# A sandwich of attention and mixture of experts on one core: three program blocks become one, six padding writes move behind the steering table, and two buffers change address

## The reference, cut to what matters

```python
# layer 1: row sums of exp(q k^T) under a causal mask, then a small MLP
o = exp_qk.sum(axis=-1)                  # one number for each token
o = relu(o @ fc1_w.T + fc1_b) @ fc2_w.T + fc2_b
# layer 2: 8 experts, each token goes to its best 2
logits = flat @ gate_w + gate_b
topv, topi = lax.top_k(logits, 2)
h = gelu(flat @ W1e + b1e); out = h @ W2e + b2e     # 256 -> 1024 -> 256
final += out * routing_weight
```

## Time and profile before

| | |
|---|---|
| time, median of 3 runs | 705.41 us (705.11 to 705.66) |
| the profiled execution: its own time, and its span | 705.67 us, 703.9 us |
| busy: PE, DVE, ACT, POOL | 563.0 (80%), 484.4 (69%), 298.3 (42%), 182.5 (26%) us |
| last input to stage 2's first matmul: last write of `steer` to first W1 matmul | 210.18 to 229.87 us |
| tiles in stage 2 | 36 |
| DMA over the whole span | 66.79 MB, 95 GB/s |

### The profile page before, as it was taken

One profiled execution on the slowest core, in us unless ns is written; L12 is line 12 of the kernel. 1 busy time (PEld: TensorE's weight loads), 2 busy tenths in 40 slices (PEclk: granted clock), 3 DMA queues, 4 the chain that ended last, 5 costly groups with the idle time before them and its releaser, 6 DMA issues. The chain is left out here.

```text
span 703.9 us, 14366 instructions
## 1 busy us (share of the span) xinstructions
PE 563.0 (80%) x4174; PEld 508.2 (72%) x4175; DVE 484.4 (69%) x1571; ACT 298.3 (42%) x673; POOL 182.5 (26%) x153
## 2 busy tenths in 40 slices
PE   2768788684230899999999999999999999999700
PEld 1536373542110899999999999999899999999600
DVE  4988888686450676976666666669766666796547
ACT  3564657564210546533333333358242424653250
POOL 2000170624424231223232323232231313131300
PEclk9958879797565899999999999999999999999955
DMA  9970020211125535632232223246432323433286
GB/s 289 310 269 0 13 102 8 83 38 53 68 70 151 188 46 152 166 44 51 39 51 39 51 39 52 38 115 163 95 45 45 45 45 45 149 55 49 46 274 211
DMA packets 52876, 66.79 MB, mean 95 GB/s; under 512 B 4870, under 2 KB 47340, under 8 KB 52716
## 3 DMA queue, kind: packets, MB, share of 16 engines
q1 hardware_dynamic: 37740, 46.81, 20.9%
q0 software_dynamic: 14016, 18.56, 15.6%
q10 hardware_dynamic: 1088, 1.07, 0.5%
HBM read 38.26 MB, written 28.74 MB: 95 GB/s over the span
## 5 line engine op out<-in xcount | busy, mean ns | idle before, releaser
L1073 ACT ACTIVATE h<-pL,b_now 128x256 f32<-128x256 f32 x288 | 121.0, 471 | 244.7 <-PE pL L1139 243.8
L1052 POOL DMA_INDIRECT sum_y<-y,dest x72 | 115.5, 1605 | 319.7 <-DVE y L1204 308.7
L1139 PE MATMUL pL<-xeT_hi,w_lo 128*128 128x256 f32 x576 | 163.5, 284 | 6.0 <-issue 3.7
L1151 PE MATMUL pY<-w_hi,h_lo 128*128 128x256 f32 x576 | 164.2, 285 | 0.9 <-DVE h_lo L1177 0.7
L1139 PE MATMUL pL<-xeT_hi,w_hi 128*128 128x256 f32 x576 | 162.5, 282 | 0.0
L1139 PE MATMUL pL<-xeT_lo,w_hi 128*128 128x256 f32 x576 | 162.4, 282 | 0.0
L1151 PE MATMUL pY<-w_hi,h_hi 128*128 128x256 f32 x576 | 161.1, 280 | 0.0
L1151 PE MATMUL pY<-w_lo,h_hi 128*128 128x256 f32 x576 | 160.8, 279 | 0.0
L1139 PEld LDWEIGHTS pL<-xeT_hi,w_lo 128*128 128x128 f32 x576 | 109.3, 190 | 7.9 <-issue 4.6
L1151 PEld LDWEIGHTS pY<-w_hi,h_lo 128*128 128x128 f32 x576 | 108.5, 188 | 1.3 <-DVE h_lo L1177 1.3
L1139 PEld LDWEIGHTS pL<-xeT_hi,w_hi 128*128 128x128 f32 x576 | 109.3, 190 | 0.0
(11 more groups left out here) (185 smaller groups left out, 699.1 us busy)
## 6 DMA issues: line engine op xcount, KB each, us to landing
w_stage<-w SPq DMA_DIRECT2D x16, 1024.0 KB, 7.9
xt<-sorted_x SPq DMA_DIRECT2D x38, 260.0 KB, 2.7
sum_y<-fill SPq DMA_DIRECT2D x1, 4352.0 KB, 24.7
w_stage<-sum_y SPq DMA_DIRECT2D x8, 512.0 KB, 5.2
out<-z SPq DMA_DIRECT2D x8, 512.0 KB, 3.0
x_all<-x SPq DMA_DIRECT2D x3, 1024.0 KB, 8.7
sum_y<-y,dest POOLq DMA_INDIRECT x72, 3.8
sorted_x<-fill ACTq DMA_DIRECT2D x4, 260.0 KB, 5.6
```

The source lines that it names most:

```text
L1052: pool.indirect_dma_start(out=sum_y, out_offset=bass.IndirectOffsetOnAxis(ap=dest[:, i:i + 1], axis=0), in_=y[:, i, :], in_offset=None, co ...
L1073: a = act.activation(h[:, c, :], pL[:, bk, i * TM:(i + 1) * TM], ACT.Gelu, bias=b1_now[par][:, c:c + 1])
L1139: mm = pe.matmul(pL[:, bk, i * TM:(i + 1) * TM], w[:, 0, col], x[:, k, :], start=(k == 0 and w is lo), stop=(k == KC - 1 and x is xeT_lo))
L1151: mm = pe.matmul(pY[:, i, 0:D], s[:, c, rows], w[:, 1, c * D:(c + 1) * D], start=(c == 0 and s is h_lo), stop=(c == FC - 1 and w is lo))
```

## The change: what it does

1. One block around all three stages. The DRAINs, gathers and releases at L336 and L999 are gone. In their place each engine waits for what it needs: PE, ACT, DVE, SP and POOL for `steer_ready` = 2 (the table's counts, L808, now increment it too), DVE also for `b2_in`, POOL for `sums_cleared`.
2. SP fills the ends of experts 0 and 1 on `ends_ready`; ACT fills those of experts 2 to 7, after `steer_ready` = 2. Nobody waits for them at once; a late tile's load waits for all 8, beside `rows_sent`.
3. A filler's 256 rows are spread so that each partition writes two neighbouring rows (`(p a)` for `(a p)`), and the ids in `fill` follow.
4. POOL sends all 16 indirect DMAs of the last batch in a row.
5. `fill` and `fwarm` live for the whole program (they were buffers of one stage); `fwarm` grows from 1 to 24 numbers for each partition. `h` is put behind `h_hi` and `h_lo`. By the addresses of the built programs, every large buffer of stages 2 and 3 keeps its address modulo 64 bytes: `w_hi1`, `w_lo1`, `xeT_hi`, `xeT_lo`, `h`, `h_hi`, `h_lo` and `z0` to `z7` were at 0 and are at 0, and the outer `w_stage`, `w_hi0`, `w_lo0`, `xt` stay at 32. In stage 1, `xn`, `xT_hi`, `xT_lo`, `qk`, `rope_a`, `rope_b`, `qkr` and `probs` go from 32 to 0, and `hid`, `hidT`, `x3T`, `logitsT` and most of the routing's small tiles from 0 to 32.

The diff, without the change of indentation and cut to its core:

```diff
+        fill = sb("fill", [P, TM // P, XW], F32)
+        fwarm = sb("fwarm", [P, 24], F32)
...
+        block = ctx.enter_context(nc.Block())
...
-            with nc.Block() as block:
-                def fill_ends(eng, experts, filled):
+            def fill_ends(eng, experts):
                     eng.wait_ge(ends_ready, 1)
                     for e in experts:
                         end = eng.value_load(steer[0:1, C_END + e:C_END + e + 1], ...)
-                        eng.dma_start(sorted_x[bass.ds(end, TM), :].rearrange("(a p) c -> p a c", p=P),
-                                      fill[:]).then_inc(filled, 16)
-                    eng.wait_ge(filled, 16 * len(experts))
+                    eng.dma_start(sorted_x[bass.ds(end, TM), :].rearrange("(p a) c -> p a c", p=P),
+                                  fill[:]).then_inc(ends_filled, 16)
...
-                    fill_ends(sp, range(0, NE, 2), ends_filled)
-                    sp.wait_ge(sums_cleared, 16)
-                    sp.wait_ge(b2_in, 16)
+                sp.sem_inc(ends_filled, ONE)
+                fill_ends(sp, range(SP_ENDS))                      # SP_ENDS = 2
...
-                    send_rows(pool, range(SENT_FIRST))
+                send_rows(pool, range(2 * TB))
...
-                    fill_ends(act, range(1, NE, 2), odd_ends_filled)
+                act.wait_ge(steer_ready, 2)
+                fill_ends(act, range(SP_ENDS, NE))
...
                     def load_tile(sp, word):
                         hold(sp, rows_sent, (word & 1) * BATCH_SENT + (B - 1) * BATCH_SENT, passed)
+                    hold(sp, ends_filled, (word & 1) * END_SENT + ONE, passed)    # END_SENT = NE * 16
...
-                    both = sp.value_load(steer[0:1, C_TILES + NE - 1:C_TILES + NE], ...)
+                sp.wait_ge(steer_ready, 2)
                     load_tile(sp, tile_word(sp, 0))
                     sp.wait_ge(tile_turned, 1)
                     sp.wait_ge(tag_saved, 1)
                     load_tile(sp, tile_word(sp, 1))
+                both = sp.value_load(steer[0:1, C_TILES + NE - 1:C_TILES + NE], ...)
...
-                    send_rows(pool, range(SENT_FIRST, 2 * TB))
+                pool.wait_ge(steer_ready, 2)
+                pool.wait_ge(sums_cleared, 16)
```

More of the change, by code:

```diff
@@ L54 @@
 BATCH_SENT = 2 * TB * 16
-SENT_FIRST = TB
+SP_ENDS = 2
+END_SENT = NE * 16
 RSQRT_LINKS = 10
@@ L931, in build @@
             xeT_lo = se("xeT_lo", [P, KC, TM], F32R)
-            h = se("h", [P, FC, TM], F32)
             h_hi = se("h_hi", [P, FC, TM], F32R)
             h_lo = se("h_lo", [P, FC, TM], F32R)
+            h = se("h", [P, FC, TM], F32)
             tag = se("tag", [P, TM // P, 4], F32)
@@ new lines, in _, with tile, first @@
+            @block.gpsimd
+            def _(pool):
+                pool.sem_inc(y_left, ONE)
+                pool.wait_ge(steer_ready, 2)
+                pool.wait_ge(sums_cleared, 16)
+                def tile(e, par, g):
+                    for i in range(TM // P):
+                        hold(pool, y_ready, 2 * g + i + 1, passed)
+                        pool.indirect_dma_start(
+                            out=sum_y, out_offset=bass.IndirectOffsetOnAxis(ap=dest[:, i:i + 1], axis=0),
+                            in_=y[:, i, :], in_offset=None,
+                            compute_op=ALU.add).then_inc(y_sent, 16)
+                    hold(pool, y_sent, (g + 1) * 32, y_left)
+                def first(e, pair, par, g):
+                    tile(e, par, g)
+                over_tiles(pool, None, first, None, tile)
@@ new lines, in tile @@
+                            for k in range(KC):
+                                col = slice(k * F + c * P, k * F + (c + 1) * P)
+                                for w, x in ((lo, xeT_hi), (hi, xeT_hi), (hi, xeT_lo)):
+                                    mm = pe.matmul(pL[:, bk, i * TM:(i + 1) * TM], w[:, 0, col], x[:, k, :],
+                                                   start=(k == 0 and w is lo), stop=(k == KC - 1 and x is xeT_lo))
+                        mm.then_inc(l1_done, 1)
+                    turn(g + 1)
```

1466 lines of the change are left out of this document (722 added, 744 removed).

## The result

The changed kernel took **700.72 us** (median of 6 runs, 698.63 to 702.19), the kernel before 705.26 (6 runs, 703.76 to 707.39): a ratio of 0.994, 95% interval 0.9925 to 0.9956. It is faster, but by 4.5 us and not by 8.9. The profiled execution took 700.91 us, with a span of 699.1 after 703.9.

The account below looks back on a forecast made before the run. POOL's drain was taken to hold up stage 2's start. 7.56 us at the hand-over and 1.34 at stage 2's end make 8.9, so 705.41 becomes 696.5 us; own range 695.0 to 697.8, 8-in-10 range 694.3 to 699.5.

Parts of the forecast that it names:

- What bounds the kernel: Between stages 1 and 2 all engines wait for POOL's drain, which ends at 222.5; stage 2's body is unchanged.
- POOL's sends: Last batch's 16 sends in a row end with a start at 224.90; tile 1 turns at 230.88, gaining 7.56 us.
- Tile 0 and ACT's fillers: At stage 2's start, six fillers free ACT at 219.9; tile 0's W1 runs 221.3 to 228.5, 2.4 us before tile 1's turn.
- ACT's fillers cost nothing: At stage 2's start, POOL's sends cover the fillers' issue; without that cover each costs 1.63 us.
- ACT becomes the later chain: Rival at stage 2's start: ACT loses over 2.4 us, giving 697.8 to 703, middle 699; chance 0.15.
- A single fetch: ACT's branch into stage 2's code might need a DMA of 2.9 us, costing 0.5 us net: 697.0.
- The end of stage 2: Into stage 3, ACT's table load and small activation move into idle time: 1.3 us saved, the wait falling from 2.32 to 1.0.
- Addresses: Buffer moves: stage 1's priced at zero; bf16 rope without a row, a tenth either way being 2 us.
- the rival "slower": Stage 2: moved `h`, `h_hi`, `h_lo` meet more conflicts; decides from 0.25 us a tile, 714.5 at 0.5 us; chance 0.05.
- if the spacing of 0.117 us moves: Sign that the prediction is wrong: PE's matmul starts in stage 2 no longer come every 0.117 us.
- the chances of "faster": Whole kernel faster by over 0.2%: 0.70, 0.15, 0.06 and half of the last, given as 0.92.

Follow-up runs that it names:

- the control: The changed kernel run once more with one unused Python constant added: 699.84 us, 0.9941 of the kernel before.
- the second pads: Four pads in the changed kernel: weights at 128 modulo 512, `xeT` at 64, `h_hi` and `h_lo` at 192; 714.09 or 712.11 us, by place of fillers.
- late fillers: The changed kernel with the second pads, its six ACT fillers still behind the steering table: 714.09 us, 0.9826 of the kernel before.
- early ones: The changed kernel with the second pads, its eight fillers four and four on SP and ACT behind the region ends: 712.11 us, 0.9814 of the kernel before.
- the padded kernels: The changed kernel with four pads moving weights, `xeT`, `h_hi` and `h_lo`: 0.984 with weights at 384 modulo 512, 0.9826 and 0.9814 at 128.
- both later probes: The changed kernel with matmul groups at 64 address pairs modulo 512 ahead of tile 0's turn, in W2's and W1's order: 0.1191 to 0.1196 us at the slowest pairs.

## Why the prediction was wrong

*What bounds the kernel: right.* The drain held the hand-over. The run with a block's end behind the sends shows it from the other side, with tile 0 loaded 7.0 us behind the last send.

*POOL's sends: right, 0.5 us short.* The last start was to be 224.90 and was 225.67: stage 1 ended 0.2 us later and the last two steps took 1.6 and 1.5 us in place of 1.27. The turn was to be 230.88 and came at 231.41; 7.56 became 7.03.

*Tile 0 and ACT's fillers: right in the result's profile and the control's.* A filler took 1.35 us in place of 1.63, W1 began at 220.20 in place of 221.3, but lasted 8.56 us in place of 7.2, since the clock was at 0.50 for longer. The idle ahead of tile 1 was 2.65 us for 2.4. "ACT's fillers cost nothing" holds in the sum there; on the other chips it cost about 2 us, by the two runs with the second pads, late fillers and early ones, whose intervals overlap. That is the rival "ACT becomes the later chain", at the place it named: ACT standing still on its way into stage 2's code. (The Trainium skill says in Runtime: NRT & Kernel Launch, section Instruction fetch mechanics, that such a branch can force a fetch. The rows show the wait of 8.22 us, and not its cause.) A single fetch, as the rival priced it, is not what the trace looks like, since instruction after instruction is slow there; what slows them stays open.

*The end of stage 2: right, a little small.* 1.34 was foretold, and the wait for ACT fell by just that, from 2.32 to 0.98, in both pairs; 1.78 and 1.55 were read in all, 1.7 was timed with the block's end put back. What is over 1.34 is an earlier landing of the first load, which nobody foretold: 3.66 and 3.89 us in place of 4.10.

*The clock: a term that was missing.* The lower level was priced only for W1 of tile 0, inside a rival. Behind the idle that the forecast itself named, 2.4 us ahead of tile 1, the clock fell in one profile, for 1.56 us, and not in the control; on another chip it fell a little earlier, for 1.56 us of tile 0's W2. The 0.18 us by which the control's interval is longer than before is not the clock: the kernel before with moved buffers has 12.12 at a clock of 1.00. A fall belonged into the range, not into the sum. That idle time brings it about is not shown; 2.5 to 2.6 us of idle went without it in three profiles.

*Addresses: the step that failed.* The sum has no term for the moves in stage 2. "So I price the moves of stage 1 at zero" was read from durations, and the rival "slower" was set aside because the earlier trace rows gave 2 ns of difference "in a busy time that is modelled". For stage 1 zero was right: first sends of successive batches are 40.8, 40.7 and 39.4 us apart before and 40.8, 40.8 and 39.5 after. The moves that mattered were those of `xeT` and `h_hi` in stage 2 (W1's 48 matmuls went from 5.56 to 5.64 us in a plain tile, W2's from 5.58 to 5.60), and what shows them is the spacing of starts, or ACT's rows by the bank. 0.105 us a tile is 1.1 ns a matmul, less than the 2 ns dismissed. Over the kernel it came to 2.4 and 3.5 us in two pairs of profiles (from tile 2's split to the last), and to 2.6 and 3.8 us where it was timed by itself. The rival's threshold, 2.6 ns, was worked out rightly; the mistake was to treat it as all or nothing, where any part of it goes into the sum. The forecast's own sign of being wrong, "if the spacing of 0.117 us moves", came true: 847 starts where there were 856. The change's own rule of 64 bytes hid this: stage 2's large buffers kept their address modulo 64, and the pace hangs on it modulo 256 and more.

*The sum corrected.* 8.9, less 0.5 for the sends and 2.4 to 3.8 for the pace, plus 0.2 to 0.4 in stage 3, is 4.8 to 6.4. 4.5 and 4.1 were timed, with intervals of 3.1 to 5.3 and 3.2 to 5.0. What is left, 0.3 to 2.3, is of the size of the clock's fall, 1.6, if some executions have it, and also within the uncertainty of the pace term and of the times; which executions had the fall can't be told from times, so this stays open. Also open is what decides between the two paces of W2 in the padded kernels, 5.42 and 5.62 us for the same 48 matmuls at the same addresses. With the second pads, at a pair that gave 0.114 in both later probes, W2 ran at the slow one in 25 of 36 tiles; the probes had neither ACT's and DVE's accesses nor an `h` tile of its own as weights.

One slip of the working: the chances of "faster" add up to 0.93 and not to 0.92; it changes nothing here.

## What to carry to other kernels

Where an engine is busy throughout, read the spacing of its starts, by a consumer's rows or by a count in a window, before and after every change that moves a buffer: 1 ns a matmul was over half of what this change won. A pad is worth trying for its own sake: pads gave 8 us in the changed kernel and 6.4 in the kernel before, about what the reordering gave. And take a block's end for what waits behind it, per place: here 7 us at one and 1.7 at the other.

## What the runs showed of the hardware that was not expected

- A 128x128 by 128x256 matmul in `fp32r` starts every 0.113 to 0.120 us at full clock, depending on where weights and moving operand begin in SBUF, up to 6% apart, with ACT, DVE and the transfers at rest.
- The same 48 matmuls at the same addresses can run at either of two paces, 0.113 to 0.114 us or 0.118, from tile to tile.
- After 2.65 us of idle, and over 1 us of new work, the granted clock fell to 0.50 for some 3 us; after 2.58 us, in the same kernel, it did not; after 1.27 and 1.12 us, in the same kernel on another chip, it did.
- 46 matmuls ahead of a loop made PE stand for 3.5 us once, some 50 us later.
- Eight DMAs of 260 KB from ACT's queue took 16.2 us to issue, the first six of them 7.1; the six of the changed kernel took 7.1 on one chip and 9.9 on another.
- On one chip ACT's sequencer took 0.70 us for a register move that took it 0.03 in a neighbouring kernel.
